# Incomplete tiles of a two-expert layer: gathered lists, stored results and finishing steps, and constant products in the router stage

## What is computed

```
x = x + conv_ref(ln_c(x), ...)          # two quantised 3x3 convolutions with batch norms
t = tokens(x)                           # (16384, 64)
flat = ln_t(t)
logits = flat @ router_w.T              # 8 experts
gates = top-2 of softmax(logits), normed to 1
h1, h3 = flat @ w1[e].T, flat @ w3[e].T # 682 hidden units, for each expert e
y = (silu(h1) * h3) @ w2[e].T
out = t + sum over the two chosen experts of gate * y
```

## Time and profile before

| | us |
|---|---|
| median of 3 runs | 1086.42 |
| lowest, highest | 1084.57, 1091.18 |
| the profiled execution | 1089.33 |
| its span, first to last instruction | 1087.3 |
| TensorE busy | 790.5 (73%) |
| VectorE busy | 574.0 (53%) |
| GpSimd busy | 465.3 (43%) |
| ScalarE busy | 434.0 (40%) |
| mean granted clock of TensorE | 0.866 |

### The profile page before, as it was taken

One profiled execution on the slowest core, in us unless ns is written; L12 is line 12 of the kernel. 1 busy time (PEld: TensorE's weight loads), 2 busy tenths in 40 slices (PEclk: granted clock), 3 DMA queues, 4 the chain that ended last, 5 costly groups with the idle time before them and its releaser, 6 DMA issues.

```text
span 1087.3 us, 20602 instructions
## 1 busy us (share of the span) xinstructions
PE 790.5 (73%) x6011; PEld 562.1 (52%) x6011; DVE 574.0 (53%) x1593; ACT 434.0 (40%) x923; POOL 465.3 (43%) x369
## 2 busy tenths in 40 slices
PE   9899678759897563655689999999999999400000
PEld 6545456526675342433467777777777777200000
DVE  6975677867775432323366776666666666200000
ACT  6254464514443121221245555666666666200000
POOL 4500467752777121121124333445444444555555
PEclk9899898989999687786899999999999999755555
DMA  7600011116663433333365656666666666111211
GB/s 224 114 7 20 34 64 64 67 38 200 169 163 87 139 92 92 107 82 114 94 171 160 157 153 177 171 161 169 179 166 160 181 173 156 11 12 11 12 10 12
DMA packets 100141, 118.80 MB, mean 109 GB/s; under 512 B 39408, under 2 KB 74480, under 8 KB 100080
## 3 DMA queue, kind: packets, MB, share of 16 engines
q1 hardware_dynamic: 64880, 102.89, 29.5%
q0 software_dynamic: 35200, 15.23, 13.2%
HBM read 96.03 MB, written 21.75 MB: 108 GB/s over the span
## 4 chain that ended last, share of the span: by engine, by line
PE 49%; SPq 14%; issue 12%; DMA 10%; DVE 8%; POOL 5%; ACT 1%; DVEq 0%; POOLq 0%; ACTq 0%
PE bank L1462 23%; PE bank L1477 13%; DMA out<-conv_all,dest_all 4%; POOL out L535 4%; SPq L429 3%; PE bank L1350 3%; DMA out<-result_rows,dest_all 2%; DMA out<-squares,dest_all 2%; SPq L427 2%; SPq L428 2%; PE bank L1368 2%; PE bank L1444 2%; SPq L406 1%; SPq L407 1%; POOL pair_rows L530 1%
## 5 line engine op out<-in xcount | busy, mean ns | idle before, releaser
L1462 PE MATMUL bank<-xT,w 64*128 64x256 f32 x1496 | 265.9, 405 | 97.4 <-DVE conv_all L1201 96.8
L1201 DVE TENSOR_TENSOR conv_all<-conv_all,bank 128x512 f32<-128x512 f32 x340 | 230.9, 686 | 151.2 <-ACT conv_all L712 150.8
L712 ACT ACTIVATE conv_all<-bank 128x512 f32<-128x512 f32 x340 | 203.1, 597 | 239.5 <-PE bank L1462 239.3
L535 POOL DMA_INDIRECT out<-conv_all,dest_all x104 | 162.4, 1561 | 250.5 <-DVE conv_all L1228 136.1
L1462 PE MATMUL bank<-xT,w_second 64*128 64x256 f32 x1496 | 245.1, 392 | 0.0
L1462 PEld LDWEIGHTS bank<-xT,w 64*128 64x128 f32 x1496 | 153.0, 195 | 152.3 <-DVE conv_all L1201 103.6
L1462 PEld LDWEIGHTS bank<-xT,w_second 64*128 64x128 f32 x1496 | 164.9, 197 | 17.7
L530 POOL DMA_INDIRECT pair_rows<-y_and_rows,slot_all x128 | 126.2, 986 | 109.3 <-DVE slot_all L1004 71.2
L1477 PE MATMUL bank<-conv_all,w 128*64 128x256 f32 x680 | 161.6, 385 | 1.4 <-DVE tile_map L1079 1.4
L1477 PE MATMUL bank<-conv_all,w_second 128*64 128x256 f32 x680 | 161.6, 385 | 0.0
L535 POOL DMA_INDIRECT out<-squares,dest_all x48 | 74.7, 1556 | 135.0 <-DVE squares L1228 83.7
(11 more groups left out here) (243 smaller groups left out, 906.2 us busy)
## 6 DMA issues: line engine op xcount, KB each, us to landing
w<-in_w SPq DMA_DIRECT2D x68, 384.0 KB, 3.0
w_second<-in_w SPq DMA_DIRECT2D x68, 384.0 KB
w<-in_w2t SPq DMA_DIRECT2D x68, 192.0 KB
w_second<-in_w2t SPq DMA_DIRECT2D x68, 192.0 KB
conv_all<-pair_rows SPq DMA_DIRECT2D x100, 68.0 KB, 1.9
x_all<-in_x SPq DMA_DIRECT2D x8, 512.0 KB, 4.3
x_all<-y_and_rows POOLq DMA_DIRECT2D x16, 256.0 KB, 3.9
out<-x_all SPq DMA_DIRECT2D x8, 512.0 KB, 2.7
```

The lines of the kernel that those rows point to most:

```text
L535: nc.gpsimd.indirect_dma_start(out, bass.IndirectOffsetOnAxis(ap=dest_all[:, j, g:g + 1], axis=0), yrow[j % RING][:, g, :], None, compute_ ...
L712: nc.scalar.activation(sbuf[k % 3], h1_ps[k % 3][:], ACT.Silu).then_inc(silu_rdy, 1)
L1201: V.tensor_tensor(hbuf[k], sbuf[k % 3], h3_ps[k % 3][:], ALU.mult).then_inc(mul_rdy, 1)
L1462: ins = mm(ps[k % 3][:, TH * of:TH * of + TH], wbuf[of][u][half, cols], xT[u][half, tokens], start=True, stop=True)
```

## The change

The slots are laid out anew: 12 unrolled, whole tiles up to 27, units in slots 28 to 55 (or whole tiles where there are fewer units), whole tiles in 56 to 67.

The lists are built otherwise. All list space is filled with pad rows by one large DMA early on. GpSimd writes pads behind each region with four wide indirect scatters (`scatter_pads`, slot 10). SyncE loads each rest into SBUF once, three in a slot (`load_rest`, slots 14 to 23), and GpSimd scatters each column of two rests into both experts' lists in blocks of four rows (`scatter_lists`, 28 scatters in slots 14 to 23).

The results of units are no longer scattered into `out`. VectorE writes them with their token number into one of four buffers, SyncE stores these next to one another in DRAM (`store_gated`), and when all lists of a pair's second expert have been worked on, a *finishing step* for that pair loads the two stretches of results (`load_finish` on SyncE), adds them (`finish` on VectorE) and scatters the sum (`finish` on GpSimd). `FINISH` sets out in which slot each of the 28 steps stands. `scatter_y` is done for every slot; for units it goes to dummy rows.

The tables for this (`rests`, `segments`, `segment_starts`, `block_rows`, `late_places`, `unit_experts`, `unit_rows`) are worked out by VectorE in tiles 6 to 12 and 24, and TensorE turns a third map in slot 24.

In the router stage TensorE multiplies constants (`keep_busy`) ahead of `positions`: 16 products in the first step, 8 in the others.

The core of the diff:

```diff
+    after = lambda b: (7 * (b + 1) + 2) // 2 if b < E - 1 else NG0
+    FINISH, at_ = {}, 0.0
+    for g_, (a_, b_) in sorted(enumerate([(a, b) for a in range(E) for b in range(a + 1, E)]), key=lambda t: t[1][::-1]):
+        at_ = max(at_ + 1 / 1.2, G0 + after(b_) + 2.0)
+        FINISH.setdefault(min(int(at_), NT), []).append((g_, G0 + after(b_)))
...
         @block.sync
+            def load_rest(g):
+                src = sp.value_load(load_map[0:1, 0, g:g + 1], min_val=0, max_val=REST - TH)
+                half = slice(64 * (g % 2), 64 * (g % 2) + 64)
+                sp.dma_start(rest_rows[half, g // 2, :], xs[bass.ds(src, TH), :].rearrange("(p g) c -> p (g c)", g=4)
+                             ).then_inc(rest_in[g // 4], 16)
+            def store_gated(j):
+                sp.wait_ge(gated_rdy, j - G0 + 1)
+                k = j - G0
+                if k:
+                    sp.wait_ge(gated_out, 16 * k)
+                sp.dma_start(yrest[2 * TH * k:2 * TH * (k + 1), :].rearrange("(t p q) r -> p t (q r)", t=2, q=2),
+                             gated[j % GR].rearrange("p (t q) r -> p t (q r)", t=2)).then_inc(gated_out, 16)
+            def load_finish(j):
+                for g, stored in FINISH.get(j, ()):
+                    n = fin[0]
+                    fin[0] += 1
+                    if n >= 2:
+                        sp.wait_ge(fin_rdy, n - 1)
+                    else:
+                        sp.wait_ge(dummy_out, 48)
+                    sp.wait_ge(gated_out, 16 * (stored - G0))
+                    for i in range(2):
+                        src = sp.value_load(load_map[0:1, 1 + i, g:g + 1], min_val=0, max_val=NU * TH)
+                        sp.dma_start(fin_in[n % 2][:, i, :, :],
+                                     yrest[bass.ds(src, TH), :].rearrange("(p g) r -> p g r", g=2)
+                                     ).then_inc(fin_rows[n % 2], 16)
-            for j in range(2, NF):
+            for j in range(2, NT):
                 if j == FULL[0]:
                     scattered(NS)
                     sp.wait_ge(tmap_rdy, 2)
-                load_rows(j, j % 2)
+                if j == G0:
+                    sp.wait_ge(tmap_rdy, 4)
+                    sp.wait_ge(lists_out, 16 * 2 * COLS)
+                if G0 <= j < G1:
+                    load_rows_apart(j, j % 2)
+                else:
+                    load_rows(j, j % 2)
                 load_weights(j, j % 2)
-                if FULL[0] <= j < FULL[0] + E + 2:
-                    gather_rests(j - FULL[0])
+                if j == 14:
+                    sp.wait_ge(load_rdy, 1)
+                    sp.wait_ge(pad_out, 64)
+                for g in range(3 * (j - 14), min(3 * (j - 13), NG)) if j >= 14 else ():
+                    load_rest(g)
+                if G0 <= j - 4 < G1:
+                    store_gated(j - 4)
+                load_finish(j - 1)
...
         @block.gpsimd
+            def scatter_pads():
+                wait_apart(pool, pad_rdy, 1)
+                for u in range(2):
+                    wait_apart(pool, scat[u], NS // 2 * 16 * GH)
+                for i in range(4):
+                    nc.gpsimd.indirect_dma_start(
+                        xs, bass.IndirectOffsetOnAxis(ap=pad_row[0:128 if i < 3 else 64, i:i + 1], axis=0),
+                        pad_rows[0:128 if i < 3 else 64].rearrange("p g r -> p (g r)"), None).then_inc(pad_out, 16)
+            def scatter_lists(c):
+                if c == 0:
+                    wait_apart(pool, block_rdy, 1)
+                    wait_apart(pool, dummy_out, 48)
+                if c % 2 == 0:
+                    wait_apart(pool, rest_in[c // 2], 64)
+                for i in range(2):
+                    nc.gpsimd.indirect_dma_start(
+                        xs_by_four, bass.IndirectOffsetOnAxis(ap=block_row[:, i, c:c + 1], axis=0),
+                        rest_rows[:, c, :], None, bounds_check=DUMMY // 4 - 1, oob_is_err=False).then_inc(lists_out, 16)
+            def finish(n):
+                u = n % 2
+                wait_apart(pool, fin_rdy, n + 1)
+                if n >= 2:
+                    wait_apart(pool, fin_out[u], 32 * (n // 2))
+                for g in range(2):
+                    nc.gpsimd.indirect_dma_start(
+                        out, bass.IndirectOffsetOnAxis(ap=fin_at[:, u, g:g + 1], axis=0),
+                        fin_sum[u][:, g, :], None, compute_op=ALU.add).then_inc(fin_out[u], 16)
-            for j in range(NF):
+            for j in range(NT + 1):
                 while rows_done < min(88 + int(4.5 * j), GH * NS):
...
-                scatter_y(j, j % 4)
-            for j in range(NF, NT):
-                scatter_y_apart(j)
+                if j < NT:
+                    scatter_y(j, j % 4)
+                if j == 10:
+                    scatter_pads()
+                while cols_done < min(int(1.5 * (j - 13)), COLS):
+                    scatter_lists(cols_done)
+                    cols_done += 1
+                for _ in FINISH.get(j, ()):
+                    finish(fins_done)
+                    fins_done += 1
...
         @block.vector
             def split(j, u, apart=0):
...
+                    V.tensor_scalar(token_f[:, j % 4, :], rows[:, :, C], 1.0, None, ALU.mult)
+                    c(V.scalar_tensor_tensor(fin_tok[:, 2, :], unit_rest[:, 2 * k:2 * k + 1].broadcast_to([128, 2]), FAR,
+                                             rows[:, 0:2, C], ALU.mult, ALU.add))
...
             def rows_out(j, v, r):
...
+                c(V.tensor_tensor(by[:, :, :, 0:C], turned, gate, ALU.mult))
+                if apart:
+                    V.tensor_copy(g[:, :, C], token_f[:, j % 4, :]).then_inc(gated_rdy, 1)
+                V.tensor_tensor(yrow[r][:, 0:2, :], g[:, 0:2, 0:C], g[:, 2:4, 0:C], ALU.add).then_inc(yr_sb, 1)
+            def finish(j):
+                for g, _ in FINISH.get(j, ()):
+                    n = fins[0]
+                    u = n % 2
+                    fins[0] += 1
+                    c = f_chain.begin(n, 2)
+                    dve.wait_ge(fin_rows[u], 16 * (n - u) + 32)
+                    if n >= 2:
+                        dve.wait_ge(fin_out[u], 32 * (n // 2))
+                    rows = fin_in[u]
+                    c(V.tensor_scalar(fin_tok[:, u, :], place_of, q2[:, 0, g:g + 1], FAR, ALU.is_ge, ALU.mult),
+                      lambda: V.tensor_tensor(fin_sum[u], rows[:, 0, :, 0:C], rows[:, 1, :, 0:C], ALU.add))
+                    c(V.tensor_tensor(fin_tok[:, u, :], fin_tok[:, u, :], rows[:, 0, :, C], ALU.add))
+                    V.tensor_tensor(fin_at[:, u, :], fin_tok[:, u, :], dummy_token[:, 4 + u, 0:2], ALU.min
+                                    ).then_inc(fin_rdy, 1)
+                    c.end()
             def between(j):
...
-                if j == 7:
+                if j == 6:
                     pad_places()
                     rests()
+                if j == 7:
+                    segments()
                 if j == 8:
-                    segments()
+                    unit_starts()
                 if j == 9:
                     segment_starts()
                 if j == 10:
-                    unit_starts()
-                if j == 11:
+                    block_rows()
+                if j == 12:
+                    late_places()
+                if j == G0 - 4:
                     unit_experts()
-                if j == 12:
                     unit_rows()
+                finish(j)
...
         @block.tensor
             def route(p, first=False, last=0):
                 if first:
+                    pe.wait_ge(raw_kept, 4)
+                    keep_busy(16, raw_ps[1])
                     positions(p)
                 if last != 1:
                     turn_rows(p + 1)
                 if last != 1:
                     raw(p + 1)
                 if not first:
+                    keep_busy(8, conv_ps[0])
                     positions(p)
...
-                if isinstance(j, int) and j == 5:
-                    turn_map(2, y_ps[:, TH:TH + 3 * SL])
-                    pe.wait_ge(tmap_rdy, 2)
+                if isinstance(j, int) and j in (5, G0 - 4):
+                    turn_map(2 if j == 5 else 3, y_ps[:, TH:TH + 3 * SL])
+                    pe.wait_ge(tmap_rdy, 2 if j == 5 else 3)
```

More of the change, by code:

```diff
@@ L323, in tiles, with loop @@
         def tiles(eng, tile):
-            first_loop = FULL[0] // 4
+            def loop(first, last, apart):
+                with eng.Fori(first // 4, last // 4) as four:
+                    for v in range(4):
+                        tile(4 * four + v, v, apart)
             for j in range(FULL[0]):
                 tile(j, j % 4, (0, 0), first=j == 0)
-            with eng.Fori(first_loop, NF // 4 - 1) as four:
-                for v in range(4):
-                    tile(4 * four + v, v, (0, 0))
+            loop(FULL[0], G0 - 4, (0, 0))
             for v in range(4):
```

(25 more changed lines are left out.)

296 lines of the change are left out of this document (169 added, 127 removed).

## The result

| | before | after |
|---|---|---|
| median, us | 1088.80 (4 runs) | 964.88 (4 runs) |
| lowest, highest | 1084.57, 1097.15 | 962.39, 966.25 |
| span of the profiled execution | 1087.3 | 962.4 |
| TensorE busy | 790.5 (73%) | 820.0 (85%) |
| granted clock, mean | 0.866 | 0.922 |

The ratio is 0.885, with a 95% interval of 0.879 to 0.891. The forecast was 946, with a main case from 920 to 975; the time is 19 us above its middle.

The account below looks back on a forecast made before the run. Bound by late row loads behind SyncE's pads and copies, and GpSimd's 151 us scatter tail. 361.1 + 463.7 + 1.5 + 3 + 4 + 4.8 + 88 = 926, GpSimd's end 947, median 946; range 882 to 975.

Parts of the forecast that it names:

- Up to tile 37: From tile 11's end at 361.12 us: 8.28 us a tile, plus 3 for pads and 1.5, 4, 4.8 for tables.
- the router: Router stage: added matmuls cost 11 us ahead of `positions` and gain at most 12 in `turn_rows`; taken as 0.
- the pads: Before tile 15's rows SyncE must wait once for GpSimd's pads to land: 3 us.
- slot 24: A second turning of the map and ten instructions of `unit_experts` and `unit_rows`: 4.8 us together.
- rival 2: Tiles 14 to 28: GpSimd's wide scatters cost by bytes and become the bound: +50 us, 996; chance 0.08.
- The stalls: Slots 46, 49, 53, 57, 58, 62, 63: VectorE waits for step n-2's landing, 8.8 us late each, 62 us together.
- The store waits: SyncE waits for freshly stored lists: 4.5 us at slots 41, 45, 48, 52 and 1 at slot 38, together 19.
- the clock: TensorE's clock is lower for a while after the finishing stage's waits: 5 us added, between 0 and 16.
- odd parts: Steps whose n-2 is two slots back land just in time or half a microsecond late: 2 us for all.
- The end: After the last tile, 926: GpSimd's remaining scatters 9.3 and 3.7 us, landing 1.4, then 6.6 to the span's end: 947.
- Rival 1: Finishing stage: landings come before VectorE asks, some 18 us in place of 88, total 876; chance 0.17.
- Rival 4: Router-stage matmuls keep the clock up, 938, or only delay `positions`, 954; inside the main case, each about one in three.

Follow-up runs that it names:

- e1: The kernel after, but GpSimd scatters the finishing steps of a slot ahead of the tile's rows instead of behind them: 888.7 us, ratio 0.812.
- e2: The kernel after with four buffers for the finishing steps in place of two, so waits are for the step four back: 892.9 us, ratio 0.817.
- e6: The kernel after with the router stage's groups of eight constant multiplications moved into the wait ahead of `turn_rows`: 954.9 us, ratio 0.874.
- e4: The kernel after without any multiplications of constants in the router stage: 961.7 us, ratio 0.880.

## Why the prediction was right, step by step

- **Up to tile 37.** Predicted end 589.7, measured 591.61. Two misses cancel most of each other, which is luck. The router stage and the first tiles ended 6.1 us later (tile 11 at 367.23, not 361.12), of which 4.3 were there at tile 0; the prediction had 0 for the router. From there on 9.1 us were lost where it had 13.3: tile 12 lost 0.9, tile 13 4.7 (4 predicted for `late_places`; the pads, 3 predicted, made no tile late), slot 24 3.3 (4.8). `block_rows` (1.5 predicted) is not among them: it ran from 359.52 to 361.21, ahead of tile 11's products, so its 1.7 us are in the 6.1. The rest went at 8.28 us a tile.
- **GpSimd's wide scatters** (rival 2): the choice of 1.0 us was right, 0.95 and 1.01 measured. GpSimd's time for a scatter does not grow with the width of its rows here.
- **The stalls.** All seven were at the slots that were named, and no others. e1 and e2 show the cause. The parts of one, in tile 47: the first scatter starts 0.89 us after `rows_out`, not 0.3, and the second half lands 3.04 us after its start; the 4.48 from the earlier trace rows were too much. So VectorE goes on 9.6 us after `rows_out` (684.36 to 693.97), where the prediction had 10.4. The seven tiles lost 10.06 us on average, 8.8 predicted.
- **The store waits.** 1.7 us at slot 38 (1 predicted) and 26.8 in the four slots with fresh lists and two steps (18). From the store's issue to the first load it was 3.56 to 3.88 us at these five slots, where the prediction had 0.5 and 1.9.
- **The step that was mis-sized is the clock.** The prediction added 5 us for the lower clock after such waits, with a bound of 16. In the kernel after, each of the eleven long waits (seven stalls and four store waits) is followed by at least sixteen products at 1.2 GHz: 695.34 to 698.92 is 3.58 us, against 660.70 to 662.53, 1.83. That is 1.75 us each, 11 x 1.75 = 19.3 us, above the bound. In nine of the eleven the lower clock lasts longer: 676.24 to the turning of the next tile's input (L1603) at 681.29 is 5.05 us, against 606.51 to 609.14, 2.63. Counted to there, the eleven cost TensorE 24.7 us. By the first count a stall without the clock is 10.06 - 1.75 = 8.3 us (8.8) and the four store waits 26.8 - 7 = 19.8 (18); with 1.7 at slot 38 (1) and 5.9 of odd parts (2) the stage's excess without the clock is 58.2 + 19.8 + 1.7 + 5.9 = 85.6 us, by the second count 80.2, where the prediction had 83. So everything but the clock adds up to within 3 us, and of the 17 us that the stage was longer the clock's miss makes 14 by the first count and all by the second. TensorE's wait at slot 38 was 1.45 us, and the products behind it ran at full clock; the eleven were of 4.23 us and more. What the half clock is worth is read from rows, and no run takes it away by itself. e1 fits: VectorE's wait fell by 64.4 us and the stage's excess by 72.7 (104.9 to 32.1), but how much of the difference is the clock's isn't shown.
- **The end.** 17.5 us from the last tile's products to the end of the span, 21 predicted. The prediction read the DMA at 1077.69 as the last one of the kernel before; it is the last in the chain, and GpSimd's timeline there has two scatters behind it:

```profile
1081.49 1.55 POOL L535 DMA_INDIRECT out<-conv_all,dest_all  x1 [2.25 <-DMA out<-conv_all,dest_all]
1083.35 1.55 POOL L535 DMA_INDIRECT out<-conv_all,dest_all  x1 [0.30 <-issue]
```

So the 6.6 us from its landing to the end of the span hold two scatters, and the sum, which adds the last slot's two scatters (3.7) and then these 6.6, counts a pair of scatters too many. That is about the 3.5 us.
- **Sum.** 1.9 + 16.9 - 3.5 = 15.3 us, and the predicted span of 947.1 becomes the measured 962.4. The time came nearer to the middle than the terms did: the shorter table work and the pair counted twice took 7.7 us off the other misses.
- **Rivals.** Rival 1 (finishing is hidden, 876) is not this kernel, but with the order of GpSimd changed it is nearly so: e1 888.7. Rival 4: in the place chosen the multiplications neither pay nor cost what could be told; where TensorE really waits they pay 6.8 us. The Trainium skill's "TensorE: Matmul & The Clock Gate", part 1, calls the throttled clock the default state, which activity releases. e6 agrees with it: with the wait filled all seven turnings took 2.02 or 2.05 us. The row that spoke against it (full clock after the longer wait) stays unexplained, and it is not alone: in the kernel after the turnings behind waits of 2.57 and 2.58 us took 2.05 and 3.25 us, and in e4 those behind 3.17 and 3.10 us took 2.05 and 3.79. What decides the clock when the wait is left empty is open.

## What to carry to other kernels

When an engine waits for the landing of something that another engine issues, look at what that engine has in its queue ahead of it, and who releases that: here VectorE waited for a scatter that stood behind one which only VectorE could release, and swapping two lines gave 76 us. A long stall of TensorE is to be priced twice, by its length and by the products at half clock after it (here 1.7 to 2.4 us behind each wait of 4.2 us and more, nothing behind one of 1.45). Filling for TensorE belongs in the wait that the trace shows ahead of the slow product: there it brought 6.8 us here, and some instructions further on nothing that could be told.

## What was not expected of the hardware

- An indirect scatter occupies GpSimd 0.95 us for rows of 4352 bytes, 1.01 for 1088 and 0.98 for 272; with adding it is 1.56 to 1.58 us for 256 bytes (means of groups).
- An adding scatter into `out` landed 3.04 us after its start in the kernel after (issued at 690.83), while TensorE and its weight loads stood still; in the kernel before, the next pair started 4.48 us after such a one while TensorE worked, and 3.80 us after one in the tail (1077.69 to 1081.49), where it stood still.
